# Attention scores from 32 array rows at a time, two heads per 32 value columns, and a block-diagonal state

## The chip, the cores and the metric

The kernel runs on one core of a Trainium2 chip. The metric is the device time of one execution in microseconds (us); the median of three is compared. TensorE, VectorE, ScalarE and GpSimd appear in the profile as PE (its weight loads as PEld), DVE, ACT and POOL; SP issues DMAs.

## What is computed

One decoder block on x of shape (4, 256, 256), all in fp32: linear attention with decay, then a mixture of four experts chosen by token, then a second attention-like layer over the batch index, each followed by a residual and a layer norm. The change is in the first part:

```
q, k = rope(silu(x@Wq)), rope(silu(x@Wk)); v = x@Wv      # 16 heads of 16, chunks of 128
scores  = einsum('bthd,bshd->bhts', qi, ki) * D          # D: causal decay
o_intra = einsum('bhts,bshd->bthd', scores, vi)
o_inter = einsum('bthd,bhde->bthe', qi*decay_q, S)
S_new   = lam_C*S + einsum('bshd,bshe->bhde', ki*decay_k, vi)
x = layernorm(x + (groupnorm(o * sigmoid(gate))*w) @ Wo)
x = layernorm(x + experts(x)); x = layernorm(x + ffn(x))
```

## The kernel before, in words

The 1024 rows of x are 8 tiles of 128, two chunks for each of the four batches. Every engine has its program written out by hand, in rounds, and the engines meet only through counting semaphores: `wait_ge(S_("probs"), n)` holds the engine's queue, with all that stands behind it, until the count is reached. Nothing reorders the work.

Round i of the attention (i from 0 to 10) works at several tiles at once. PE: `transpose_qk(i)`, `attend(i-1)`, in even rounds `make_state`, `proj_qkv(i+1)` (queries and keys together, then values), in round 7 (`MOE_START`) `transpose_h(0)`, the scores of tile i, `transpose_on(i-2)`, `turn_back(i-1)`, `project_o(i-2)`. DVE: `copy_kT(i)`, `gate_o(i-2)` and `norm_o(i-2)` (a chain of some 13 small instructions, of which eleven are the inverse root `newton`/`ors`), in even rounds `decay_state`, a layer norm (`h`), `rope_cos(i+1)` (`rcos`), four `mask_scores` (`probs`) with `rope_add(i+1)` (`qkr`) between the second and the third, `residual1(i-2)` (`x`, `stats`, `agg`). In round 3 and in round 5 DVE also prepares weights of the last part behind its residual (with `f_w`). ACT: `expand_q(i)`, `silu_qk(i+1)`, `copy_v(i+1)`, `copy_oT(i-1)`, `copy_onT(i-2)`.

A score matmul takes all 128 array rows, that is the keys of eight heads, against `qx`, the queries expanded with zeros so that only one head meets its keys; one covers four heads (512 columns). The four of a tile alternate between PSUM banks 3 and 4, so the third needs the first mask, the fourth the second. Values are padded from 16 to 32 columns per head, so outputs and state hold 32 rows or columns per head, half of them zero. `attend` keeps four heads in flight, each in its own 32 array columns, and begins with group g as soon as that group's mask is done. From round 7 on rounds of the experts are mixed in (`expert_up`, `expert_down`; `hTe` and `aTe` are their masked inputs). In round 8 `attend(7)` stands on PE between `expert_up(0)` and `expert_up(1)`.

Of the kernel before, what the change touches and what calls it, by code (L numbers as in the profile page):

```python
# [39 lines left out]
C_CHUNK = C_PARITY + 2  # L40
C_ROPE2 = C_CHUNK + KT
C_TRIL = C_ROPE2 + L * 2 * HK
C_POW = C_TRIL + L * L * H
C_END = C_POW + 1
# [14 lines left out]
def shape_constants():  # L59
# [6 lines left out]
    for f in range(KT):  # L66
        c[:, C_CHUNK + f] = np.exp(-slope * P)[f * (H // KT) + p // HD]

# [19 lines left out]
def decoder_block(nc, x, tokens, ctx, wq, wk, wv, wo, wg1, wg2, norm_w, conv_w, fwq, fwk, fwv, fwg, router, fwout,  # L88
                  consts, out):
    stack = ExitStack()  # L90
    with stack:
# [45 lines left out]
        qx = sb("qx", [P, 2, KT, 8, P])  # L137
        kT = sb("kT", [P, 2, KT, P])
        probs = sb("probs", [P, 2, H, P])
        state = sb("state", [P, KT, D])  # L140
# [24 lines left out]
        after = qx[:, :, :, :, :].rearrange("p b k h n -> p (b k h n)")  # L165
        fq = after[:, 0:1024].rearrange("p (c l n) -> p c l n", c=2, l=L)
        fv = after[:, 2048:4096].rearrange("p (c l n) -> p c l n", c=2, l=L)
# [36 lines left out]
        tril = con[:, C_TRIL:C_TRIL + L * L * H].rearrange("p (l m h) -> p l m h", l=L, m=L)  # L204
        half_neg = con[:, C_POW:C_POW + 1]

# [53 lines left out]
        def _(eng):  # L260
            eng.memset(qx[:, :, :, :, :], 0.0).then_inc(S_("zeros"), 1)
# [206 lines left out]
        def _(eng):  # L468
# [7 lines left out]
            eng.wait_ge(S_("zeros"), 2)  # L476
# [7 lines left out]
            def copy_v(i):  # L484
                eng.wait_ge(S_("v_made"), i + 1)
                if i >= 3:
                    eng.wait_ge(S_("o_made"), i - 2)
                    eng.wait_ge(S_("state_made"), (i - 3) // 2 + 1)
                eng.activation(v_sb[:, i % 3, :, 0:HD], heads(bank[1][:, 0:D]), ACT.Copy).then_inc(S_("v_copied"), 1)

            def expand_q(i):
                eng.wait_ge(S_("qkT_made"), i + 1)
# [3 lines left out]
                for r in range(4):  # L496
                    rr = slice(32 * r, 32 * r + 32)
                    for par in range(2):
                        eng.activation(qx[rr, i % 2, :, 2 * r + par, :], two(bank[2][rr, 0:2 * P]), ACT.Copy,  # L499
                                       scale=con[rr, C_PARITY + par:C_PARITY + par + 1]).then_inc(S_("q_expanded"), 1)  # L500

            def copy_oT(i):
# [3 lines left out]
                eng.activation(oT[:, i % 2, :], bank[5][:, :], ACT.Copy).then_inc(S_("oT_copied"), 1)  # L506
# [125 lines left out]
        def _(eng):  # L632
# [74 lines left out]
            def copy_kT(i):  # L707
                eng.wait_ge(S_("kT_made"), i + 1)
                if i >= 2:
                    eng.wait_ge(S_("scores_made"), 4 * (i - 1))  # L710
                eng.tensor_copy(kT[:, i % 2, :, :], two(bank[7][:, 0:D])).then_inc(S_("kT_copied"), 1)

            def mask_scores(i, g):
                eng.wait_ge(S_("scores_made"), 4 * i + g + 1)
                if i >= 2:
                    eng.wait_ge(S_("o_made"), i - 1)
                eng.tensor_tensor(probs[:, i % 2, 4 * g:4 * g + 4, :],  # L717
                                  bank[3 + g % 2][:, :].rearrange("p (h n) -> p h n", h=4),
                                  causal.unsqueeze(1).to_broadcast([P, 4, P]), ALU.mult).then_inc(S_("probs"), 1)

            def decay_state(b):
# [3 lines left out]
                for f in range(KT):  # L725
# [633 lines left out]
```

## Time and profile before

| | |
|---|---|
| median of three executions | 255.02 us (254.4, 255.02, 258.87) |
| span of the profiled execution, first to last instruction | 256.0 us |
| mean granted TensorE clock, share of full speed | 0.925 |
| busy: PE, DVE, POOL, ACT | 82%, 69%, 45%, 32% of the span |

The profiled execution's own device time is not listed apart; its span lies 1.0 us above the median. "Busy" of PE counts matmuls in flight, so it does not say that PE sets the pace. An fp32 matmul appears as two records, each with a weight load; a transpose is one record. In the timeline, records of one kind are merged, and in brackets stands how long the engine had been idle before and which work ended last ahead of it ("issue" where the profile shows none).

### The profile page before, as it was taken

The page shows a single profiled execution, that of the slowest core. Times are in us where ns is not written, and L with a number is a line of the kernel's source. Part 1 is how long each engine was busy: PE and PEld are TensorE (multiplying, and loading weights), DVE is VectorE, ACT ScalarE, POOL GpSimd, SP SyncE. Part 2 cuts the span into 40 slices and gives each one's busy share as a digit, 9 for nine tenths or more (in the row PEclk, how much of TensorE's full clock was granted, in tenths as well). Part 3 has the DMA queues.
Part 4 walks back from the last instruction along what each step waited for, and adds up shares of the span by engine and source line. Part 5 has one row for each costly group of instructions (what it writes and reads, how often), then busy time and mean ns, then how long its engine had stood idle before and what let it go on. Part 6 is the DMA issues. An engine that isn't in the chain of part 4 may idle for free.

```text
span 256.0 us, 3809 instructions
## 1 busy us (share of the span) xinstructions
PE 209.2 (82%) x1254; PEld 146.0 (57%) x1254; DVE 176.7 (69%) x438; ACT 81.7 (32%) x219; POOL 114.0 (45%) x188
## 2 busy tenths in 40 slices
PE   3788999995987798849799989999999997842461
PEld 1367555562745364515799776686786966411340
DVE  1168848779597979793556863348769788897751
ACT  0075664452432534241100113403223234423021
POOL 9661207335161413140516352346558529656352
PEclk9999999999799999977979999999999999995555
DMA  7990000000000000000000000000000001001011
GB/s 195 339 299 5 3 0 4 0 1 0 3 1 0 3 1 0 3 0 0 3 0 3 1 0 0 3 1 0 0 3 0 0 4 40 3 0 41 0 38 45
DMA packets 7027, 6.65 MB, mean 26 GB/s; under 512 B 1232, under 2 KB 6624, under 8 KB 7008
## 3 DMA queue, kind: packets, MB, share of 16 engines
q1 hardware_dynamic: 5744, 5.33, 6.6%
q10 hardware_dynamic: 1264, 1.08, 1.4%
q8 instruction: 10, 0.16, 0.3%
q14 instruction: 9, 0.07, 0.1%
HBM read 5.36 MB, written 1.05 MB: 25 GB/s over the span
## 4 chain that ended last, share of the span: by engine, by line
PE 52%; DVE 24%; issue 9%; POOL 6%; ACT 4%; DMA 3%; ACTq 1%; DVEq 0%; POOLq 0%
PE bank L1029 19%; PE bank L1230 12%; PE bank L1087 9%; PE bank L1244 4%; PE bank L1024 3%; DMA w_qk<-in_L_attn_Wk 3%; DVE hTe L776 2%; DVE w_qk L937 2%; PE bank L1132 2%; DVE stats L749 1%; POOL rstd L301 1%; DVE newton L685 1%; DVE probs L717 1%; PE bank L1120 1%; DVE newton L684 1%
## 5 line engine op out<-in xcount | busy, mean ns | idle before, releaser
L1087 PE MATMUL bank<-qx,kT 128*128 128x512 f32 x64 | 33.7, 652 | 10.6 <-DVE probs L717 8.9
L1230 PE MATMUL bank<-hTe,ctxT 128*128 128x128 f32 x256 | 31.7, 285 | 2.6 <-issue 2.6
L1230 PEld LDWEIGHTS bank<-hTe,ctxT 128*128 128x128 f32 x256 | 31.0, 201 | 3.2 <-issue 3.1
L499 ACT ACTIVATE qx<-bank,con 32x256 f32<-32x256 f32 x64 | 26.4, 458 | 16.0 <-PE bank L1024 15.4
L1244 PE MATMUL bank<-ctxT,aTe 128*128 128x256 f32 x128 | 29.0, 379 | 0.0
L284 POOL TENSOR_TENSOR rsin<-qk,rope_tab 128x256 f32<-128x256 f32 x16 | 13.2, 845 | 34.9 <-ACT qk L482 34.9
L1029 PE MATMUL bank<-f_w,oT 128*128 128x512 f32 (+4 forms) x80 | 28.0, 496 | 0.8 <-ACT oT L552 0.7
L298 POOL TENSOR_SCALAR rstd<-agg 128x1 f32<-128x1 f32 x24 | 5.3, 222 | 49.3 <-DVE agg L751 48.5
L1087 PEld LDWEIGHTS bank<-qx,kT 128*128 128x128 f32 x64 | 11.7, 197 | 26.8 <-issue 24.5
L717 DVE TENSOR_TENSOR probs<-bank,con 128x512 f32<-128x512 f32 x32 | 21.6, 686 | 5.8 <-PE bank L1087 5.0
L1244 PEld LDWEIGHTS bank<-ctxT,aTe 128*128 128x128 f32 x128 | 23.7, 190 | 2.9
L336 POOL TENSOR_TENSOR aTe<-rcos,mask 128x256 f32<-128x256 f32 x8 | 11.9, 1493 | 25.5 <-DVE rcos L835 25.5
L1029 PEld LDWEIGHTS bank<-f_w,oT 128*128 128x128 f32 x80 | 14.4, 190 | 12.0 <-issue 5.7
L835 DVE TENSOR_TENSOR rcos<-rcos,bank 128x256 f32<-128x256 f32 x8 | 3.4, 420 | 21.7 <-ACT rcos L602 21.7
L1029 PE MATMUL bank<-w_qk,xT 128*128 128x512 f32 x32 | 17.0, 658 | 1.5 <-DMA w_qk<-in_L_attn_Wk 1.5
L301 POOL TENSOR_TENSOR rstd<-rstd,con 128x1 f32<-128x1 f32 x24 | 14.0, 582 | 2.0
L336 POOL TENSOR_TENSOR hTe<-hT,mask 128x512 f32<-128x512 f32 x8 | 13.3, 1656 | 2.6 <-ACT hT L539 2.6
L1024 PE MATMUL bank<-con,fgo 128*128 128x128 f32 x16 | 3.7, 357 | 12.8 <-POOL fgo L414 12.8
L512 ACT ACTIVATE onT<-bank 128x256 f32<-128x256 f32 x8 | 3.1, 384 | 33.8 <-PE bank L1024 33.8
L1029 PE MATMUL bank<-f_out,onT 128*128 128x256 f32 x32 | 11.7, 522 | 1.6 <-ACT onT L592 1.6
L1024 PEld LDWEIGHTS bank<-con,fgo 128*128 128x128 f32 x16 | 2.4, 179 | 15.2 <-POOL fgo L414 14.8
L1111 PE MATMUL bank<-probs,v_sb 128*32 128x128 f32 x256 | 10.8, 274 | 0.0
(128 smaller groups left out, 407.7 us busy)
## 6 DMA issues: line engine op xcount, KB each, us to landing
x_sb<-in_x SPq DMA_DIRECT2D x4, 256.0 KB, 6.8
ctx_sb<-in_ctx SPq DMA_DIRECT2D x1, 1024.0 KB, 12.3
out<-x_sb SPq DMA_DIRECT2D x8, 128.0 KB, 1.7
fgo<-in_itok_BxS ACTq DMA_DIRECT2D x1, 512.0 KB, 9.3
con<-shape_constants SPq DMA_DIRECT2D x1, 338.5 KB, 3.0
w_v<-in_L_attn_Wv SPq DMA_DIRECT2D x1, 256.0 KB, 5.5
w_qk<-in_L_attn_Wq ACTq DMA_DIRECT2D x1, 256.0 KB, 5.7
w_qk<-in_L_attn_Wk ACTq DMA_DIRECT2D x1, 256.0 KB, 7.3
```

The source lines that it names most:

```text
L284: eng.tensor_tensor(dst[:, :, s, :], src[:, :, 1 - s, :], tab[:, :, s, :], ALU.mult)\
L298: eng.tensor_scalar(rstd[:, n, i:i + 1], agg[:, n, i, 1:2], LN_EPS, None, ALU.add)\
L301: eng.tensor_tensor(rstd[:, n, i:i + 1], rstd[:, n, i:i + 1], half_neg, ALU.pow)\
L336: eng.tensor_tensor(dst[:, j % 2, experts[0]:experts[1], :, :], two(src[:, j % 2, :]).unsqueeze(1).to_broadcast([P, n, KT, P]), mask[:, ex ...
L499: eng.activation(qx[rr, i % 2, :, 2 * r + par, :], two(bank[2][rr, 0:2 * P]), ACT.Copy, scale=con[rr, C_PARITY + par:C_PARITY + par + 1]). ...
L717: eng.tensor_tensor(probs[:, i % 2, 4 * g:4 * g + 4, :], bank[3 + g % 2][:, :].rearrange("p (h n) -> p h n", h=4), causal.unsqueeze(1).to_ ...
L1024: last = eng.transpose(dst[:, k * P:(k + 1) * P], src[:, k * P:(k + 1) * P], ident)
L1029: last = eng.matmul(dst, lhsT[:, k, :], w[:, k, :], start=(k == 0), stop=(k == KT - 1))
L1087: eng.matmul(bank[3 + g % 2][:, :], kT[:, i % 2, g // 2, :], qx[:, i % 2, g // 2, 4 * (g % 2):4 * (g % 2) + 4, :].rearrange("p h n -> p (h ...
L1111: last = eng.matmul(bank[5][32 * n:32 * n + 32, g * P:(g + 1) * P], v_sb[:, i % 3, h, :], probs[:, i % 2, h, :], start=(i % 2 == 0), stop= ...
L1230: last = eng.matmul(bank[0][:, f * P:(f + 1) * P], ctxT[:, k, e, f * P:(f + 1) * P], hTe[:, j % 2, e, k, :], start=(e == 0 and k == 0), st ...
L1244: last = eng.matmul(bank[3][:, 0:D], aTe[:, j % 2, e, k, :], ctxT[:, k, e, :], start=(e == 0 and k == 0), stop=(e == E - 1 and k == KT - 1))
```

## The change

- `expand_q` writes two copies of the transposed queries (one for even, one for odd heads of each pair), with 2 instructions on 128 partitions in place of 8 on 32. `qx` shrinks from 8 to 2 planes and needs no clearing; the buffers of the last part that lay over it get a tensor of their own (`after`).
- A score matmul takes the 32 array rows of two heads (strip r, half f) against the two parities (256 columns). There are 8 per tile; strips 0, 1 and 2 write banks 3, 4 and 7 without waiting for a mask of this tile, strip 3 reuses bank 3 behind the first mask.
- Values of two heads share 32 columns (`packed`), so the output and the state are dense: `attend` takes its state part with 4 matmuls of full size in place of 16 of 32 columns, `copy_oT` copies 256 columns, `turn_back` makes two transposes in place of four and puts them in the upper half of bank 5, and `decay_state` is one instruction with a block mask. The table of constants grows by 254 columns.
- Waits: the transposed keys lie in bank 2 beside the queries, so `expand_q` waits for both and `copy_kT` for `expand_q`. The state lies in bank 1 beside the values, so the value projection waits for `decay_state`. `attend` waits for all four masks and for `gate_o` of the tile before, which now stands first in DVE's round.

```diff
             def expand_q(i):
-                eng.wait_ge(S_("qkT_made"), i + 1)
+                eng.wait_ge(S_("kT_made"), i + 1)
...
-                for r in range(4):
-                    rr = slice(32 * r, 32 * r + 32)
-                    for par in range(2):
-                        eng.activation(qx[rr, i % 2, :, 2 * r + par, :], two(bank[2][rr, 0:2 * P]), ACT.Copy,
-                                       scale=con[rr, C_PARITY + par:C_PARITY + par + 1]).then_inc(S_("q_expanded"), 1)
+                for par in range(2):
+                    eng.activation(qx[:, i % 2, :, par, :], two(bank[2][:, 0:D]), ACT.Copy,
+                                   scale=con[:, C_PARITY + par:C_PARITY + par + 1]).then_inc(S_("q_expanded"), 1)
...
             def copy_kT(i):
                 eng.wait_ge(S_("kT_made"), i + 1)
+                eng.wait_ge(S_("q_expanded"), 2 * i + 2)
...
             def decay_state(b):
...
-                for f in range(KT):
-                    eng.tensor_scalar(state[:, f, :], bank[7][:, f * D:(f + 1) * D], con[:, C_CHUNK + f:C_CHUNK + f + 1],
-                                      None, ALU.mult).then_inc(S_("state"), 1)
+                eng.tensor_tensor(state[:, :], bank[1][:, D:2 * D], chunk_decay, ALU.mult).then_inc(S_("state"), 1)
...
             def attention_round(i):
+                if 0 <= i - 2 < TILES:
+                    gate_o(i - 2)
                 if i < TILES:
                     copy_kT(i)
...
-                if i >= 3:
-                    eng.wait_ge(S_("gated"), i - 2)
+                if i:
+                    eng.wait_ge(S_("state"), (i + 1) // 2)
                 project(bank[1][:, 0:D], xt, w_v[:, :, :]).then_inc(S_("v_made"), 1)
...
+            def score_rows(i, r, f):
+
+                rr = slice(32 * r, 32 * r + 32)
+                return eng.matmul(score_bank(r)[:, f * D:(f + 1) * D], kT[rr, i % 2, f, :],
+                                  qx[rr, i % 2, f, :, :].rearrange("p h n -> p (h n)"), start=True, stop=True)
...
+                for f in range(KT):
+                    for r in range(3):
+                        last = score_rows(i, r, f)
+                        if f == KT - 1:
+                            last.then_inc(S_("scores_made"), 1)
+                eng.wait_ge(S_("probs"), 4 * i + 1)
+                for f in range(KT):
+                    last = score_rows(i, 3, f)
+                last.then_inc(S_("scores_made"), 1)
...
             def attend(i):
...
-                    eng.wait_ge(S_("oT_copied"), i)
+                    eng.wait_ge(S_("gated"), i)
```

On PE, from the state matmuls of tile 4 to the scores of tile 6, which is round 6 up to its scores. Before:

```order
L1120 MATMUL bank<-v_sb,qkr 128x256 [waits v_copied,kT_copied]
L1120 MATMUL bank<-v_sb,qkr 128x256
L1029 MATMUL bank<-w_qk,xT 128x512 [waits qk_silu]
L1029 MATMUL bank<-w_qk,xT 128x512
L1029 MATMUL bank<-w_v,xT 128x256 [waits gated,v_copied]
L1029 MATMUL bank<-w_v,xT 128x256
L1087 MATMUL bank<-qx,kT 128x512 [waits probs,kT_copied,q_expanded] x4
```

And in the changed kernel:

```order
L1142 MATMUL bank<-v_sb,qkr 128x128 [waits v_copied]
L1142 MATMUL bank<-v_sb,qkr 128x128
L1040 MATMUL bank<-w_qk,xT 128x512 [waits qk_silu]
L1040 MATMUL bank<-w_qk,xT 128x512
L1040 MATMUL bank<-w_v,xT 128x256 [waits state,v_copied]
L1040 MATMUL bank<-w_v,xT 128x256
L1091 MATMUL bank<-qx,kT 128x256 [waits probs,kT_copied,q_expanded]
L1091 MATMUL bank<-qx,kT 128x256 x5
L1091 MATMUL bank<-qx,kT 128x256 [waits probs]
L1091 MATMUL bank<-qx,kT 128x256
```

The value projection (`w_v`) now waits for DVE's `state` of the same round, and the last two score matmuls for the first mask.

On PE in round 8, `attend(7)` between the experts' first up-projection and their second. Before, its last two groups of heads and what follows:

```order
L1106 MATMUL bank<-qx,state 32x128 [waits probs]
L1106 MATMUL bank<-qx,state 32x128 x3
L1111 MATMUL bank<-probs,v_sb 32x128 x4
L1106 MATMUL bank<-qx,state 32x128 [waits probs]
L1106 MATMUL bank<-qx,state 32x128 x3
L1111 MATMUL bank<-probs,v_sb 32x128 x4
L1024 MATMUL bank<-con,h 128x128 [waits hT_copied,h1_done]
L1024 MATMUL bank<-con,h 128x128
L1230 MATMUL bank<-hTe,ctxT 128x128 [waits activated,hTe_pool,hTe_vector]
```

And in the changed kernel, from `expert_up(0)` (the first two rows) to `expert_up(1)` (the last):

```order
L1246 MATMUL bank<-hTe,ctxT 128x128 [waits qk_silu,hTe_pool,hTe_vector]
L1246 MATMUL bank<-hTe,ctxT 128x128 x15
L1129 MATMUL bank<-qx,state 128x128 [waits state,probs,v_copied,gated]
L1129 MATMUL bank<-qx,state 128x128
L1133 MATMUL bank<-probs,v_sb 32x128 x8
L1129 MATMUL bank<-qx,state 128x128 x2
L1133 MATMUL bank<-probs,v_sb 32x128 x8
L1035 MATMUL bank<-con,h 128x128 [waits probs,hT_copied,h1_done]
L1035 MATMUL bank<-con,h 128x128
L1246 MATMUL bank<-hTe,ctxT 128x128 [waits activated,hTe_pool,hTe_vector]
```

`attend` (L1129, L1133; its first state matmul waited for `state,probs,v_copied,oT_copied` before) has changed the wait on ACT's copy for `gated`; everything below it on PE's queue waits with it. What it waits for stands on DVE, in the changed kernel, at the change from round 7 to round 8:

```order
L846 TENSOR_TENSOR rcos<-rcos,bank 128x256 [waits z_silu]
L786 TENSOR_TENSOR aTe<-rcos,mask 128x768 [waits activated]
L786 TENSOR_TENSOR hTe<-hT,mask 128x512 [waits hT_copied]
L744 TENSOR_TENSOR og<-bank,gate 128x256 [waits o_normed,o_back]
L765 TENSOR_SCALAR h<-x,agg,rstd 128x256 [waits ln0_rstd]
L748 TENSOR_TENSOR osq<-og 128x256 [waits gated]
```

`og` (`gate_o`) stands one instruction earlier than before, ahead of `h`, but still behind the three expert instructions.

## Rows read from the trace of the kernel before

**Rows 1.** The page: granted clock (tenths) and DMA rate in 40 slices; the constants' DMA.
```profile
PEclk9999999999799999977979999999999999995555
GB/s 195 339 299 5 3 0 4 0 1 0 3 1 0 3 1 0 3 0 0 3 0 3 1 0 0 3 1 0 0 3 0 0 4 40 3 0 41 0 38 45
...
con<-shape_constants SPq DMA_DIRECT2D x1, 338.5 KB, 3.0
```

**Rows 2.** Timeline, DVE in round 5: start us, us, engine, line, operation.
```profile
81.99 0.42 DVE L762 TENSOR_TENSOR x<-bank,x_sb 128x256 f32<-128x256 f32 x1 [1.13 <-PE bank L1029]
...
83.33 0.41 DVE L733 TENSOR_TENSOR og<-bank,gate 128x256 f32<-128x256 f32 x1
...
89.12 1.27 DVE L717 TENSOR_TENSOR probs<-bank,con 128x512 f32<-128x512 f32 x2
...
93.75 0.42 DVE L762 TENSOR_TENSOR x<-bank,x_sb 128x256 f32<-128x256 f32 x1 [1.13 <-PE bank L1029]
```

**Rows 3.** Timeline, PE and ACT in round 5.
```profile
82.21 3.37 ACT L499 ACTIVATE qx<-bank,con 32x256 f32<-32x256 f32 x8 [1.44 <-PE bank L1024]
...
86.02 1.88 PE L1087 MATMUL bank<-qx,kT 128*128 128x512 f32 x4
...
89.94 1.96 PE L1087 MATMUL bank<-qx,kT 128*128 128x512 f32 x4 [2.04 <-DVE probs L717]
...
92.58 1.13 PE L1029 MATMUL bank<-w_o,onT 128*128 128x256 f32 x4
```

**Rows 4.** Timeline, round 6 up to its first mask, PE and DVE.
```profile
94.08 0.43 PE L1106 MATMUL bank<-qx,state 128*32 128x128 f32 x8
...
96.66 0.41 DVE L733 TENSOR_TENSOR og<-bank,gate 128x256 f32<-128x256 f32 x1
96.79 1.13 PE L1120 MATMUL bank<-v_sb,qkr 128*128 128x256 f32 x4 [0.76 <-DVE kT L711]
...
97.76 1.88 PE L1029 MATMUL bank<-w_qk,xT 128*128 128x512 f32 x4
...
100.19 0.87 DVE L726 TENSOR_SCALAR state<-bank,con 128x256 f32<-128x256 f32 x2
100.34 1.88 PE L1087 MATMUL bank<-qx,kT 128*128 128x512 f32 x4
...
102.43 1.27 DVE L717 TENSOR_TENSOR probs<-bank,con 128x512 f32<-128x512 f32 x2
```

**Rows 5.** Timeline, rounds 3 and 4: late scores, residual, gate, first mask.
```profile
61.84 1.27 DVE L717 TENSOR_TENSOR probs<-bank,con 128x512 f32<-128x512 f32 x2
62.66 2.38 PE L1087 MATMUL bank<-qx,kT 128*128 128x512 f32 x4 [2.83 <-DVE probs L717]
...
67.85 0.42 DVE L762 TENSOR_TENSOR x<-bank,x_sb 128x256 f32<-128x256 f32 x1 [2.09 <-PE bank L1029]
...
71.22 0.41 DVE L733 TENSOR_TENSOR og<-bank,gate 128x256 f32<-128x256 f32 x1
...
77.35 1.27 DVE L717 TENSOR_TENSOR probs<-bank,con 128x512 f32<-128x512 f32 x2
```

**Rows 6.** Half-microsecond windows: busy of PE, PEld, DVE, ACT, POOL, granted clock, DMA.
```profile
64.50:65.00 0.50, 0.50 (x2) 0.16 (x1) 0.00 (x0) 0.00 (x0) 0.00 (x0) 0.50 0.00 0
```

**Rows 7.** Timeline, DVE and PE at the change from round 0 to round 1.
```profile
33.28 1.46 DVE L717 TENSOR_TENSOR probs<-bank,con 128x512 f32<-128x512 f32 x2
...
34.37 1.08 PE L1111 MATMUL bank<-probs,v_sb 128*32 128x128 f32 x32
```

**Rows 8.** Timeline, rounds 7 and 8.
```profile
120.64 3.74 PE L1230 MATMUL bank<-hTe,ctxT 128*128 128x128 f32 x32
...
124.31 0.43 PE L1106 MATMUL bank<-qx,state 128*32 128x128 f32 x8
...
126.16 1.22 DVE L776 TENSOR_TENSOR hTe<-hT,mask 128x512 f32<-128x512 f32 x1
...
128.60 5.44 PE L1230 MATMUL bank<-hTe,ctxT 128*128 128x128 f32 x32 [1.97 <-issue]
```

More of the change, by code:

```diff
@@ L136, in decoder_block @@
         v_sb = sb("v_sb", [P, 3, H, 32])
-        qx = sb("qx", [P, 2, KT, 8, P])
+        qx = sb("qx", [P, 2, KT, 2, P])
+        after = sb("after", [P, 3 * L * D])
         kT = sb("kT", [P, 2, KT, P])
         probs = sb("probs", [P, 2, H, P])
-        state = sb("state", [P, KT, D])
+        state = sb("state", [P, D])
         oT = sb("oT", [P, 2, 512])
@@ L1099, in attend @@
                 if i % 2:
-                    eng.wait_ge(S_("state"), 2 * (i // 2) + 2)
-                for g in range(4):
-                    eng.wait_ge(S_("probs"), 4 * i + g + 1)
+                    eng.wait_ge(S_("state"), i // 2 + 1)
+                eng.wait_ge(S_("probs"), 4 * i + 4)
+                for f in range(KT):
+                    out = bank[5][:, f * P:(f + 1) * P]
                     if i % 2:
-                        for n in range(4):
-                            h = 4 * g + n
-                            eng.matmul(bank[5][32 * n:32 * n + 32, g * P:(g + 1) * P],
-                                       state[:, h // 8, 32 * (h % 8):32 * (h % 8) + 32],
-                                       qx[:, i % 2, h // 8, h % 8, :], start=True, stop=False)
-                    for n in range(4):
-                        h = 4 * g + n
-                        last = eng.matmul(bank[5][32 * n:32 * n + 32, g * P:(g + 1) * P], v_sb[:, i % 3, h, :],
-                                          probs[:, i % 2, h, :], start=(i % 2 == 0), stop=True)
+                        for par in range(2):
+                            eng.matmul(out, state[:, f * P:(f + 1) * P], qx[:, i % 2, f, par, :],
+                                       start=(par == 0), stop=False, skip_group_check=True)
+                    for par in range(2):
+                        for r in range(4):
+                            last = eng.matmul(out[32 * r:32 * r + 32, :], v_sb[:, i % 3, 8 * f + 2 * r + par, :],
+                                              probs[:, i % 2, 4 * r + 2 * f + par, :],
+                                              start=(i % 2 == 0 and par == 0), stop=(par == 1), skip_group_check=True)
                 last.then_inc(S_("o_made"), 1)
@@ L1116, in make_state @@
                 i = 2 * b
-                eng.wait_ge(S_("kT_copied"), i + 1)
                 eng.wait_ge(S_("v_copied"), i + 1)
                 for f in range(KT):
-                    last = eng.matmul(bank[7][:, f * D:(f + 1) * D], qkr[:, i % 2, D + f * P:D + (f + 1) * P],
-                                      v_sb[:, i % 3, 8 * f:8 * f + 8, :].rearrange("p h e -> p (h e)"),
-                                      start=True, stop=True)
+                    last = eng.matmul(bank[1][:, D + f * P:D + (f + 1) * P], qkr[:, i % 2, D + f * P:D + (f + 1) * P],
+                                      packed(v_sb[:, i % 3, 8 * f:8 * f + 8, :]), start=True, stop=True)
                 last.then_inc(S_("state_made"), 1)
@@ L1127, in turn_back @@
                 eng.wait_ge(S_("oT_copied"), i + 1)
-                eng.wait_ge(S_("v_copied"), min(i + 3, TILES))
-                if i:
-                    eng.wait_ge(S_("gated"), i)
-                for g in range(4):
-                    last = eng.transpose(bank[1][:, g * P:(g + 1) * P], oT[:, i % 2, g * P:(g + 1) * P], ident)
-                last.then_inc(S_("o_back"), 1)
+                transpose2(bank[5][:, D:2 * D], oT[:, i % 2, 0:D]).then_inc(S_("o_back"), 1)
             proj_qkv(0)
@@ L1170, in attention_round @@
                 if i < TILES:
-                    for g in range(4):
-                        scores(i, g)
+                    scores(i)
                 if 0 <= i - 2 < TILES:
```

69 lines of the change are left out of this document (37 added, 32 removed).

## The prediction

> **What bounds the kernel now.** I read the page first: PE is busy 82% of the span, DVE 69%, and PE's clock is full except in a few slices [rows 1]. The shares don't say what the change is worth, so I read the timeline of the attention, round by round, for what each engine waits for. From round 3 on it is one loop between DVE and PE. X is where the residual `x` starts, M where the first mask starts. In round 5 [rows 2]: X at 81.99, M at 89.12, the next X at 93.75. From X to M (7.13) DVE works almost without a gap: statistics, gate, inverse root, layer norm, `rcos`. From M to X (4.63) PE sets the time: it has been idle 2.04 us for the first mask [rows 3], then come two scores of 512 columns, a transpose and its copy, and the output projection from 92.58, and DVE waits 1.13 us for it. So the scores made ahead of M cost nothing there, those behind M all of their time, and every instruction on DVE ahead of M costs its own.
>
> **Late scores: a gain in each round.** Behind M stand 2 matmuls of 512 columns, 0.86 us each (four records from 89.94 to 91.65, [rows 3]). In their place come 2 of 256 columns in the same array strip, which can't run together: half, 0.86 in all. Nothing else of the path from M to X changes: the two transposes saved in `turn_back` (0.22) lie beside ACT's copy of `onT`. So M to X shrinks by 0.86, and DVE still waits 0.3 at X, since its four masks and `qkr` are done some 3.5 us after M.
>
> **Early scores.** Six matmuls of 256 columns in three strips. If the strips run together they take 0.86, one after another 2.57. Column strips do run together here: 16 matmuls of 32 columns by 128 take 1.08 us [rows 7], where one after another, at 0.86 x 128/512 = 0.21 each, they would take 3.4. Row strips appear nowhere in this trace. Their weights are 128 columns wide and each fp32 matmul loads twice; the nearest row is `expert_up`, 32 pairs of a 128-column load and a 128-column pass in 3.67 us (120.64 to 124.31, [rows 8]), 0.115 a pair. I can't tell load from pass in it, so a load is at most 0.115. Twelve loads in sequence bound the six at 1.4. I take 1.3 (the first mask can start 1.1 after the first of them, plus 0.2 for the hand-over) and keep both ends.
>
> The Trainium skill (TensorEngine Tiling (Array Packing), Key Properties) says that different tiles can load and multiply in parallel; by that rule it is 0.86, a rival below. TensorE: Matmul & The Clock Gate, LDWEIGHTS, says that a load costs its columns whatever its rows, a 32x128 load as much as a 128x128 one. That speaks for 1.3. No row here shows either alone.
>
> **The query copies and the order on DVE.** ACT's eight `qx` instructions take 3.37 us [rows 3], two of them 0.84. They start 0.22 later, behind the transposes of k, so are done 1.3 us after X; the gate stands first and fills DVE until about then. `copy_kT` behind it costs no more than ahead of it. Zero in odd rounds. The 3.37 us are hidden today, since scores wait for M, so their saving is worth nothing in itself.
>
> **Even rounds 4 and 6: two new waits on PE.** `attend` now waits for the gate, and the value projection for the state. Round 6, counted from X at 93.75 ([rows 4]). The gate now starts where `kT` did, 0.34 ahead of 96.66, so at X+2.6, and ends at X+3.0 (the extra weights of the last part stand before it). Attend takes 1.9 (94.08 to 96.79 less 0.76 idle), to X+4.95; its state part is 4 full matmuls of 0.21 for 4 groups of 0.22, no difference. `make_state` halves, 0.97 to 0.48, X+5.4. Queries and keys 1.72, X+7.15. On DVE the inverse root ends and `state` starts at X+6.45 (3.53 behind the gate, plus 0.34 for `kT`), ends X+6.9, 0.45 sooner for being one instruction; so the value wait is just covered. Values 0.86, X+8.0. Scores 1.1 + 0.1, hand-over 0.2: M at X+9.5, against 8.68 today (102.43). So +0.8, less 0.86 behind M. In round 4 the same sum with the gate at X+3.0 (71.22 - 67.85 less 0.34) gives M at X+9.95 against 9.5 [rows 5]: +0.45, less 0.86. Together -0.5. If the six scores took 2.57, the first mask would wait for four of them, 1.71, +0.6 in each round.
>
> **Odd rounds.** Rounds 5 and 7: -0.86 each, -1.7. Round 3: -0.86, and the clock. Today PE idles 2.83 us before the late scores, and then works at 0.50 of the clock, the 1.2 GHz level [rows 6], so that M to X is 6.01 in place of 4.63 [rows 5]. With the gate wait, the idle time is split into 1.2 and 2.4, and I take that the fall stays out there: -1.4. Round 3: -2.3.
>
> **Rounds 0 to 2,** where PE is the busier one: in round 0 `copy_kT` waits for ACT (1.1 us where the transposes alone took 0.2), the four `ctxT` copies behind it slide by 0.9, and behind them state, values (they wait for it), scores and masks. Then `attend(0)`, which starts at 34.37 while two masks run [rows 7], waits for all of them, until 34.75. Packed scores give back 1.71 - 1.2 in each. I reckon M of round 2 at 1.2 late, and 0.86 back behind it: +0.3.
>
> **Round 8: the dearest new wait.** Today `attend(7)` runs from 124.31, in the shadow of DVE's and POOL's masked inputs, and `expert_up(1)` starts at 128.60. Now it waits for `gate_o(6)`, which stands on DVE behind `hTe` (126.16 + 1.22) and ends at 127.85. Attend 1.9, two transposes 0.2: `expert_up(1)` at 130.0, +1.4 [rows 8]. It is on the path, and behind it so is everything.
>
> **Constants.** 254 more columns, 130 KB, at the 339 GB/s of the start [rows 1] 0.4 us, ahead of the weights that PE waits for: +0.3. GpSimd loses the clearing of `qx`, which nothing waits for, 0.
>
> **Clock lost elsewhere.** The new idle stretches are about 3.1 and 2.7 us before attend in rounds 4 and 6 and 3.5 in round 8, against the 2.83 that cost 1.4. In round 8 `expert_up(1)` ran slow already (5.44 against 3.67), so there the fall only changes its victim. For rounds 4 and 6 I charge one fall, +1.3.
>
> **The sum:** +0.3 - 2.3 - 0.5 - 1.7 + 1.4 + 0.3 + 1.3 = -1.2. Against the profiled span, 256.0 - 1.2 = 254.8; it lies 1.0 above the median, so **253.8**.
>
> **Rivals.**
> - Strips load and multiply at once, and the clock holds. Early scores 0.86 in place of 1.3, in the five rounds 0, 1, 2, 4 and 6: -2.0; no charge for the clock, -1.3; and round 8 keeps the full clock, so the 1.8 of the slow `expert_up(1)` comes back in part, -0.9. 249.6. For it: the column strips. Against it: longer idle stretches than today.
> - The strips don't run together (the change doesn't do what it says): +0.6 to +0.7 in those five rounds, +3.2: 257.0. For it: no row shows row strips. Against: column strips do.
> - The other side: the gate wait cools PE. What counts is not the wait but the work behind it: attend, `make_state`, `qk` and values (5 us at full speed) stand right behind the idle stretch and ahead of M. Let the clock fall at each of the waits of rounds 4, 6 and 8 and in round 3 again, each for the 1.4 that round 3 shows today: rounds 4 and 6 2.8 in place of the 1.3 charged, +1.5; round 3 +1.4; round 8 +1.4 if `expert_up(1)` stays slow as well. +4.3: 258.1. It decides at the length of the stretch: behind 2.83 us the fall came [rows 5, 6], behind the 2.04 of round 5 [rows 3] it didn't, and the new ones are 2.7 to 3.5.
>
> **How the numbers follow.** Forecast 253.8 at 0.5, its own range 251.5 to 256 (0.1 a round either way in the hand-overs, one fall of the clock more or less). Fast rival 0.2, no overlap 0.13, cold PE 0.17. The range 249.3 to 258.6 leaves out the tails beyond the outer rivals. A measurement of this kernel tells about 2%, 5.1 us, from no change (its three runs span 4.5): faster by that is below 249.9, most of the fast rival and no more, 0.15; slower is above 260.1, half of the cold rival and a little of the others, 0.1; within 0.75.
>
> **What the profile after would show.** Late scores 0.86 behind M and X 3.8 behind M; six early scores in 1.3 (0.86 and 2.57 are the rivals); PE idle 3 us before attend in rounds 4 and 6, put down to `og`; M 9.5 and 9.95 behind X there; `attend(7)` at 127.8 less what was gained, released by `og`; ACT 2.5 us less per tile with no change of time from it. It would be wrong if the experts' part moved by more than the shift at its start, or if the masks became the bound behind M.

## The result and the profile after

The changed kernel took **269.42 us** (median; 267.03 to 270.87) against 254.82 (254.4 to 258.87) of the kernel before on the same chip, a ratio of **1.054** [1.045, 1.062]: slower, outside the range of 249.3 to 258.6. The profiled execution took 268.65 with a span of 266.8, against 256.0 before. Executions of one kernel differ by up to 3%, and a ratio counts only those within 1.5% of the kernel's fastest, so medians over all executions stand beside the ratios. The span of 256.0 belongs to the longest of the first three executions of the kernel before (258.87; the other two, 254.4 and 255.02, are shorter than that span, while in all other runs here the device time is 1.7 to 3.0 longer than the span). So "before" in a trace stands for a long execution, at a mean clock of 0.925, where later executions of this kernel have 0.921 to 0.945, most of them above 0.93.

The page of the changed kernel: PE's busy share and clock in 40 slices, and three groups of instructions (busy us, mean ns | idle before them and its releaser):

```profile
PE   2798887987668886874949999899999998761552
...
PEclk9999979779779777978688999999999999995657
...
L1091 PE MATMUL bank<-qx,kT 32*128 32x256 f32 x128 | 19.1, 408 | 11.1 <-DVE probs L730 10.6
...
L1129 PE MATMUL bank<-qx,state 128*128 128x128 f32 x32 | 8.5, 411 | 9.3 <-DVE og L744 9.3
...
L1133 PE MATMUL bank<-probs,v_sb 128*32 128x128 f32 x256 | 13.0, 350 | 2.8 <-DVE og L744 2.2
```

Two things are new against [rows 1]. The clock has dips in every round, from slice 6 on; in the first three of these slices PE is busy for 80% or more. And `attend` (L1129, L1133) waits 11.5 us for `og`.

The whole attention in windows (busy of PE, PEld, DVE, ACT, POOL, then the granted clock), after:

```profile
22.00:142.00 120.00, 93.92 (x634) 63.09 (x633) 80.01 (x202) 21.45 (x51) 35.70 (x60) 0.83 0.00 1
```

and before:

```profile
22.00:128.00 106.00, 90.92 (x677) 55.55 (x675) 80.50 (x191) 43.10 (x100) 34.78 (x59) 0.95 0.00 1
```

DVE's busy time is the same and ACT's is halved, as meant; PE's busy time grew although it has less to do, since it works at 0.83 of its clock in place of 0.95. In half-microsecond windows from 22 us to the end of the experts' second up-projection (145.85, before 134.04) I count those that read below 0.75: 11 stretches (36 to 39, 46 to 49.5, 56.5 to 59.5, 70 to 73.5, 77 to 80 and so on), 40.0 us in all; before it was 3, from 64.0, 112.0 and 129.0, 13.5 us in all. The 26.5 us more cost at most half their length, 13.3.

The first of them is in round 0. Timeline, PE and DVE:

```profile
31.95 1.14 PE L1091 MATMUL bank<-qx,kT 32*128 32x256 f32 x12
33.12 1.29 DVE L730 TENSOR_TENSOR probs<-bank,con 128x512 f32<-128x512 f32 x2 [1.01 <-PE bank L1091]
33.86 1.13 PE L1091 MATMUL bank<-qx,kT 32*128 32x256 f32 x4 [0.77 <-DVE probs L730]
...
36.35 1.93 PE L1133 MATMUL bank<-probs,v_sb 128*32 128x128 f32 x32 [0.64 <-DVE probs L730]
```

and windows of the scores and of what follows:

```profile
31.50:35.00 3.50, 2.72 (x19) 1.48 (x17) 2.49 (x5) 0.38 (x1) 1.84 (x2) 1.00 0.00 0
...
36.00:39.00 3.00, 2.65 (x33) 2.01 (x34) 0.63 (x2) 0.59 (x2) 0.00 (x0) 0.50 0.00 0
```

The scores ran at full clock, six matmuls in the same 1.14 us as the late two (1.13): the strips run together, and the first mask started 1.17 after the first of them. Then the clock fell, and `attend(0)` took 1.93 for what took 1.08 before [rows 7]. The idle stretches around it are new but short: 1.18 us at 27.3 (0.35 before), 0.77 and 0.64, where the kernel before idled for 2.04 us in round 5 and kept its clock [rows 1], [rows 3].

Rounds 3 and 4:

```profile
68.19 1.13 PE L1091 MATMUL bank<-qx,kT 32*128 32x256 f32 x4 [2.31 <-DVE probs L730]
...
70.16 2.08 PE L1040 MATMUL bank<-w_o,onT 128*128 128x256 f32 x4 [0.25 <-ACT onT L524]
...
72.28 0.42 DVE L772 TENSOR_TENSOR x<-bank,x_sb 128x256 f32<-128x256 f32 x1 [1.74 <-PE bank L1040]
...
75.30 0.41 DVE L744 TENSOR_TENSOR og<-bank,gate 128x256 f32<-128x256 f32 x1
...
75.77 0.71 PE L1129 MATMUL bank<-qx,state 128*128 128x128 f32 x4 [2.68 <-DVE og L744]
```

The late scores shrank as forecast, but the output projection behind them took 2.08 in place of 1.13 [rows 3], so M to X is 4.82 in round 3 and 5.02 in round 5, where 3.8 was forecast. Round 8:

```profile
130.20 4.32 PE L1246 MATMUL bank<-hTe,ctxT 128*128 128x128 f32 x32
...
137.44 0.41 DVE L744 TENSOR_TENSOR og<-bank,gate 128x256 f32<-128x256 f32 x1
...
137.91 0.94 PE L1129 MATMUL bank<-qx,state 128*128 128x128 f32 x4 [3.39 <-DVE og L744]
...
142.11 3.74 PE L1246 MATMUL bank<-hTe,ctxT 128*128 128x128 f32 x32
```

`attend(7)` stands behind `og`, and with two transposes it takes 4.2 us, most of it at 0.50 of the clock. The second up-projection starts 13.5 later than before (142.11 against 128.60 [rows 8]); 2.7 of it come back from there on: 1.7 in the up-projection itself, which took 3.74 in place of 5.44, since the third stretch of before lay on it, and the rest behind it, where the clock stood higher in two of the last four slices (5657 against 5555).

### The profile page after: what moved, and what is told of

Its sections match the earlier page's. It is cut to its first block, busy times and chain, and to the rows that moved or that the text cites. A ratio compares the mean times of both kernels' runs of the same rounds, so it can differ in the third digit from the quotient of the medians.

```text
span 266.8 us, 3622 instructions
## 1 busy us (share of the span) xinstructions
PE 210.1 (79%) x1206; PEld 151.5 (57%) x1206; DVE 171.9 (64%) x434; ACT 60.4 (23%) x171; POOL 111.0 (42%) x187
## 3 DMA queue, kind: packets, MB, share of 16 engines
q10 hardware_dynamic: 1264, 1.08, 1.3%
## 4 chain that ended last, share of the span: by engine, by line
PE 53%; DVE 24%; POOL 7%; issue 7%; ACT 4%; DMA 3%; ACTq 1%; DVEq 0%; POOLq 0%
PE bank L1040 21%; PE bank L1246 11%; PE bank L1091 5%; PE bank L1035 4%; PE bank L1260 4%; PE bank L1133 3%; PE bank L1129 3%; DMA w_qk<-in_L_attn_Wk 3%; DVE probs L730 3%; DVE w_qk L948 2%; DVE hTe L786 2%; POOL rstd L313 2%; DVE stats L759 1%; ACT onT L524 1%; DVE rcos L707 1%
## 5 line engine op out<-in xcount | busy, mean ns | idle before, releaser
L296 POOL TENSOR_TENSOR rsin<-qk,rope_tab 128x256 f32<-128x256 f32 x16 | 14.3, 913 | 48.6 <-ACT qk L494 48.6
L1246 PE MATMUL bank<-hTe,ctxT 128*128 128x128 f32 x256 | 30.5, 278 | 0.2 <-issue 0.2
L1091 PE MATMUL bank<-qx,kT 32*128 32x256 f32 x128 | 19.1, 408 | 11.1 <-DVE probs L730 10.6
L348 POOL TENSOR_TENSOR aTe<-rcos,mask 128x256 f32<-128x256 f32 x8 | 11.9, 1493 | 27.9 <-DVE rcos L846 27.9
L730 DVE TENSOR_TENSOR probs<-bank,con 128x512 f32<-128x512 f32 x32 | 20.5, 682 | 4.4 <-PE bank L1091 4.4
L1091 PEld LDWEIGHTS bank<-qx,kT 32*128 32x128 f32 x128 | 11.5, 188 | 17.7 <-DVE probs L730 13.8
L1129 PE MATMUL bank<-qx,state 128*128 128x128 f32 x32 | 8.5, 411 | 9.3 <-DVE og L744 9.3
L1040 PE MATMUL bank<-w_o,onT 128*128 128x256 f32 x32 | 14.4, 597 | 1.5 <-ACT onT L524 1.2
L1133 PE MATMUL bank<-probs,v_sb 128*32 128x128 f32 x256 | 13.0, 350 | 2.8 <-DVE og L744 2.2
L348 POOL TENSOR_TENSOR hTe<-hT,mask 128x512 f32<-128x512 f32 x8 | 13.3, 1658 | 1.4 <-ACT hT L551 1.4
L1129 PEld LDWEIGHTS bank<-qx,state 128*128 128x128 f32 x32 | 6.3, 278 | 11.8 <-DVE og L744 10.4
L707 DVE TENSOR_TENSOR rcos<-qk,rope_tab 128x512 f32<-128x512 f32 x8 | 6.5, 808 | 10.0 <-ACT qk L494 10.0
## 6 DMA issues: line engine op xcount, KB each, us to landing
x_sb<-in_x SPq DMA_DIRECT2D x4, 256.0 KB, 7.7
w_v<-in_L_attn_Wv SPq DMA_DIRECT2D x1, 256.0 KB, 6.4
w_qk<-in_L_attn_Wq ACTq DMA_DIRECT2D x1, 256.0 KB, 6.4
w_qk<-in_L_attn_Wk ACTq DMA_DIRECT2D x1, 256.0 KB, 8.0
```

Source lines behind the costliest of these rows:

```text
L296: eng.tensor_tensor(dst[:, :, s, :], src[:, :, 1 - s, :], tab[:, :, s, :], ALU.mult)\
L348: eng.tensor_tensor(dst[:, j % 2, experts[0]:experts[1], :, :], two(src[:, j % 2, :]).unsqueeze(1).to_broadcast([P, n, KT, P]), mask[:, ex ...
L707: eng.tensor_tensor(rcos[:, i % 2, :], qk[:, i % 2, :], rope_tab[:, i % 2, 0, :], ALU.mult)\
L730: eng.tensor_tensor(probs[:, i % 2, 4 * g:4 * g + 4, :], score_bank(g)[:, :].rearrange("p (h n) -> p h n", h=4), causal.unsqueeze(1).to_br ...
L1040: last = eng.matmul(dst, lhsT[:, k, :], w[:, k, :], start=(k == 0), stop=(k == KT - 1))
L1091: return eng.matmul(score_bank(r)[:, f * D:(f + 1) * D], kT[rr, i % 2, f, :], qx[rr, i % 2, f, :, :].rearrange("p h n -> p (h n)"), start= ...
```

## Experiments

Two theories stood before the first of these runs: **rows**, that matmuls over few array rows let the clock fall; **wait**, that the new wait of `attend` for `og` does, as the cold-PE rival had it.

### Both kernels with the other's score matmuls

The changed kernel, with matmuls over all 128 rows in place of strips:

```diff
-                return eng.matmul(score_bank(r)[:, f * D:(f + 1) * D], kT[rr, i % 2, f, :],
-                                  qx[rr, i % 2, f, :, :].rearrange("p h n -> p (h n)"), start=True, stop=True)
+                return eng.matmul(score_bank(r)[:, f * D:(f + 1) * D], kT[:, i % 2, f, :],
+                                  qx[:, i % 2, f, :, :].rearrange("p h n -> p (h n)"), start=True, stop=True)
```

> The changed kernel with each group of 32-row score matmuls replaced by one matmul of all 128 rows and the same 256 columns: two early (four in round 0), two late. It leaves out part of the scores (banks 4 and 7 keep old values, heads are mixed), with all masks, waits and later work in place, so its time stands for the same schedule with full array rows. Theory A (32-row matmuls count too little as work, and the clock falls behind them): the clock stays near 1.0 in rounds 0 to 2, falls at most in rounds 3, 4, 6, 7 and 8 behind the long waits, mean clock at or above 0.92, time 256 to 261. Theory B (the falls come from the new idle stretches): the same falls as the changed kernel, mean clock 0.86 to 0.89, time 267 to 270.

The kernel before, with its score matmuls over 32 rows:

```diff
-                eng.matmul(bank[3 + g % 2][:, :], kT[:, i % 2, g // 2, :],
-                           qx[:, i % 2, g // 2, 4 * (g % 2):4 * (g % 2) + 4, :].rearrange("p h n -> p (h n)"),
+                eng.matmul(bank[3 + g % 2][:, :], kT[0:32, i % 2, g // 2, :],
+                           qx[0:32, i % 2, g // 2, 4 * (g % 2):4 * (g % 2) + 4, :].rearrange("p h n -> p (h n)"),
```

> The kernel before, with its four score matmuls per tile over array rows 0 to 31 in place of all 128 (it leaves out three quarters of each sum); columns, order and waits as before. Theory A: the clock falls in most rounds of the attention, mean clock below 0.90, time 262 or more against 255. Theory B: nothing changes, 255 and clock 0.925.

And the same over 64 rows (`kT[0:64]`, `qx[0:64]`), run later:

> The kernel before with its four score matmuls per tile over array rows 0 to 63 (half of each sum left out). Rows in flight: between, 259 to 264, clock 0.89 to 0.91. Only the lone strip: 255, clock 0.925.

Measured: full rows in the changed kernel 259.81 (254.54 to 262.2), ratio to the kernel before 1.001 [0.993, 1.009]. That ratio rests on three executions of ten; the medians over all, 259.81 and 256.93, give 1.011. So four fifths of the loss or more are gone. 32 rows in the kernel before 269.25 (267.65 to 270.0), 1.049 [1.040, 1.057]; 64 rows 262.86, 1.027 [1.019, 1.034]. Nothing else was touched there: instructions, columns, waits and order are those of the kernel before. Round 1 of the 32-row version, windows of its eight score records and of what follows:

```profile
38.50:42.40 3.90, 3.88 (x10) 1.27 (x9) 3.27 (x5) 0.96 (x3) 3.56 (x6) 1.00 0.00 0
...
43.00:46.00 3.00, 3.00 (x45) 2.53 (x47) 1.90 (x6) 2.21 (x6) 0.86 (x3) 0.50 0.03 8
```

PE was busy for 3.88 of the 3.90 us and without a gap in the second, and the clock stood at 0.50 there, where the kernel before has 1.00. That shows **rows**: fewer rows in the scores, and nothing else, give the kernel before a loss of the size of the change, and with 64 rows a good half of it stays (0.027 of 0.049).

The full-row version settles round 0 as well. It has nearly the same idle stretches there as the changed kernel, and `attend(0)` behind them took 1.08:

```profile
33.95 1.13 PE L1090 MATMUL bank<-qx,kT 128*128 128x256 f32 x4 [0.79 <-DVE probs L730]
...
36.44 1.08 PE L1132 MATMUL bank<-probs,v_sb 128*32 128x128 f32 x32 [0.63 <-DVE probs L730]
```

Rounds 0 to 2 in one window, the changed kernel and then the one with full rows:

```profile
22.00:62.00 40.00, 33.44 (x238) 22.03 (x236) 24.78 (x53) 9.66 (x21) 10.55 (x18) 0.87 0.00 1
...
22.00:62.00 40.00, 32.36 (x226) 21.84 (x224) 28.41 (x64) 10.89 (x24) 14.46 (x28) 1.00 0.00 1
```

The full-row trace is of one of its longest executions (262.07), and still shows no dip there; its dips come from 64 us on.

### The gate moved ahead of the next residual

`gate_o` of a tile goes behind the four masks of the round before, so that `attend` finds it done:

```diff
             def attention_round(i):
-                if 0 <= i - 2 < TILES:
+                if i == TILES + 1:
                     gate_o(i - 2)
...
+                if 1 <= i < TILES:
+                    gate_o(i - 1)
                 if 0 <= i - 2 < TILES and i < TILES:
                     residual1(i - 2)
```

> The changed kernel with gate_o of tile i-1 moved into round i, between the masks and the residual, where DVE waits for PE, so that attend does not wait for it. Theory A: the waits for og (11.5 us in all) go, 4 to 7 us come back, and the falls of the clock behind the scores stay: 262 to 265, clock below 0.91. Theory B (idle stretches and these waits are the whole of it): the long idle stretches before attend are gone and with them most falls, 253 to 257.

And with the full-row matmuls as well:

> The early gate with every score matmul over all 128 rows, 256 columns, two early (four in round 0) and two late; it leaves out part of the scores, as the run with full rows did. It bounds what a full array and the early gate are worth together: 247 to 251 if the clock is what is left of the loss after the early gate; 259 to 262 if it is not.

Measured: 260.85 (259.34 to 264.57), 1.015 [1.002, 1.028]; with full rows 255.24 (252.12 to 258.73), 0.994 [0.989, 0.998]. So the wait costs time too, some 10 us by the ratios (1.054 to 1.015), but the two don't add: full rows alone give 12 to 13.5 back, the gate alone some 10, both some 15. Most of the dips stay in the version with the gate alone (34.5 us in place of 40.0, by the same windows), without any wait for `og`. What became late next is the wait that the prediction had found just covered: the value projection for `state`:

```profile
78.63 2.04 PE L1042 MATMUL bank<-w_v,xT 128*128 128x256 f32 x4 [2.70 <-DVE state L738]
```

### TensorE alone

A kernel with no other work: PE multiplies without a pause, 28 steps of 256 columns with all rows, then 28 steps of each kind (one strip of 32 rows; three; four; one of 64; two of 64; four column strips), with 28 full steps between them.

> TensorE alone: phases of 28 fp32 matmuls of 128 rows by 256 columns (12 us), and between them phases of as many steps of 1, 3, 4 strips of 32 rows, 1 and 2 strips of 64 rows, and 4 strips of 32 columns. It computes nothing of the block. Theory A: the granted clock falls to 0.5 in the phase of one 32-row strip although PE is never idle, and stays 1.0 with 4 strips and with 2 of 64 rows; 3 strips and 1 of 64 rows show where between. Theory B: 1.0 throughout. Strips in flight together: 28 steps of 3 or 4 take about the 12 us of the full phases; if loads come one after another, 28 x 6 x 0.107 = 18 us for three and 24 us for four.

Windows inside the phases, in that order (busy of PE, PEld, POOL, then the clock):

```profile
26.00:46.00 20.00, 20.00 (x48) 15.04 (x47) 0.00 (x0) 0.51 0.00 1
57.00:69.00 12.00, 12.00 (x166) 10.73 (x161) 0.00 (x0) 1.00 0.01 3
81.00:93.00 12.00, 12.00 (x225) 11.34 (x224) 0.00 (x0) 1.00 0.01 3
106.00:118.00 12.00, 12.00 (x57) 10.14 (x56) 0.00 (x0) 1.00 0.01 1
130.00:142.00 12.00, 12.00 (x111) 10.69 (x112) 0.00 (x0) 1.00 0.00 1
155.00:166.00 11.00, 11.00 (x212) 6.62 (x208) 0.00 (x0) 1.00 0.01 3
```

One strip alone took the clock to 0.51 although PE is never idle. Three and four strips make 166 and 225 records in the time of 57, so they run fully side by side, weight loads too, and keep the clock. The Trainium skill (TensorEngine Tiling (Array Packing), Key Properties) says that different tiles load and multiply in parallel; this trace agrees. The Trainium skill (TensorE: Matmul & The Clock Gate, What's actually happening) has the gate follow how busy PE is; the first window differs from that, PE busy all the time at 0.51, and the measurement decides.

Mixtures, also without a pause: two strips and two in turn; one and three; one and two; three times one strip and then a full matmul; two and two.

> TensorE never idle, computing nothing of the block: phases of 32 steps of 256 columns between full phases of 28, with 2 strips of 32 rows in each step (mean 64 rows), 1 and 3 in turn (64), 1 and 2 in turn (48), three steps of 1 to one full (56), two of 1 to two full (80). By rows in flight the clock falls first in the phase of 48 and stays in that of 80; if only a lone strip counts too little, the first phase stays at 1.0 and those with many lone strips fall (the fourth before the third).

```profile
22.00:34.00 12.00, 12.00 (x114) 10.65 (x114) 0.00 (x0) 1.00 0.01 1
48.00:60.00 12.00, 12.00 (x116) 10.71 (x115) 0.00 (x0) 1.00 0.01 1
80.00:96.00 16.00, 16.00 (x57) 12.92 (x55) 0.00 (x0) 0.50 0.00 0
120.00:136.00 16.00, 16.00 (x34) 10.16 (x35) 0.00 (x0) 0.50 0.00 0
147.00:161.00 14.00, 14.00 (x54) 8.91 (x54) 0.00 (x0) 1.00 0.01 1
```

The clock follows the mixture, not its emptiest part: one strip and three hold it as two and two do, one and two don't. The last window shows one cost more, which the forecast left out: 54 records in 14.00 us at full clock, where full rows alone would make some 66 (57 in 12.00), so a step from a strip to full rows or back costs some 0.2 us (an estimate, 27 steps of 0.52 for 0.43 with a passage at every second). In the changed kernel the first score starts 0.96 behind the value projection (40.53 to 41.49), with full rows 0.86 (39.27 to 40.13): small beside the clock.

A third kernel of this kind, bursts of two steps and a wait for DVE between them, was to show the same with idle time:

> TensorE in bursts of two steps of 256 columns (0.86 us), each followed by a wait for one small VectorE instruction (some 0.6 us), 16 bursts to a phase; it computes nothing of the block. Phases of full rows stand between phases of 4, 3 and 2 strips of 32 rows in flight, one of 64 rows, one of 32 rows. If the monitor counts rows in flight: full rows and 4 strips keep 1.0, one strip falls to 0.5, 2 strips and 64 rows behave alike (fall), 3 strips in between. If it counts instructions or time in flight: all phases alike.

It tells nothing on rows. Already its full-row bursts took 2.07 us. In the blocks above four such records take 1.13 behind a wait at full clock (`w_o` [rows 3]) and 2.08 at 0.50 (70.16):

```profile
9.27 2.07 PE L132 MATMUL bank<-x_sb 128*128 128x256 f32 x4 [0.59 <-DVE junk L118]
```

so by its durations it ran at the low level from its start, and there was nothing to fall from.

### Which of the scores

Strips 0 and 1 ahead of the first mask and 2 and 3 together behind it, in place of three and one:

```diff
-                    for r in range(3):
+                    for r in range(2):
                         last = score_rows(i, r, f)
...
-                    last = score_rows(i, 3, f)
-                last.then_inc(S_("scores_made"), 1)
+                    for r in range(2, 4):
+                        last = score_rows(i, r, f)
+                        if f == KT - 1:
+                            last.then_inc(S_("scores_made"), 1)
```

> The changed kernel with the strips of 32 rows issued in two pairs: strips 0 and 1 early (banks 3 and 4), strips 2 and 3 together behind the first mask (banks 7 and 3), so that no strip is ever alone in the array. Late time unchanged (two steps of 256 columns). If the lone strip is what lets the clock fall: most of the 12 to 14 us come back, 257 to 262. If strips count by rows, as the fewer rows early take back what the late ones give (0.43 us x 3 + 0.86 x 1 against 0.86 x 2 + 0.86 x 2 of row time): 266 to 270, as the changed kernel. If only idle stretches count: 269.

and with the early gate:

> Both edits: strips in pairs and gate_o(i-1) ahead of the residual of round i. If each repairs a cause of its own: 250 to 256, faster than either alone (260.9 for the early gate). If the pairs repair nothing: 259 to 262.

Only the late two over all rows:

```diff
                 for f in range(KT):
-                    last = score_rows(i, 3, f)
+                    last = full_rows(i, 3, f)
```

> The changed kernel with only the two late matmuls over all 128 rows (their scores mix heads), the six early strips as they are: the six leave 96 of 128 rows busy. If the lone late strip is the cause: 255 to 261, as with full rows everywhere (fast runs 255). If the early strips count too little as well: 263 to 268.

Measured: pairs 269.11 (267.9 to 271.32), 1.052 [1.043, 1.060], no change from three and one; with the early gate 262.56 (258.08 to 263.32), no interval, against 260.85 with three and one. Late full rows 258.58 (257.69 to 259.91), 1.011 [1.006, 1.016]. So two matmuls in a tile make some 11 us of the loss (0.043 of 0.054), but sharing the same strips out more evenly gives nothing, as one and three held the clock as two and two did on TensorE alone.

Can the late pair be filled up with zeros? The queries of strip 3 are copied once more with the other rows set to zero, and the late matmuls take all rows, with the early gate. First with the keys' copy held behind two more ACT instructions, then with that off the path (the second copy made from `qx`):

```diff
+                for par in range(2):
+                    eng.activation(qz[:, i % 2, :, par, :], two(bank[2][:, 0:D]), ACT.Copy,
+                                   scale=con[:, C_LAST + par:C_LAST + par + 1]).then_inc(S_("q_last"), 1)
...
-                    last = score_rows(i, 3, f)
+                    last = eng.matmul(score_bank(3)[:, f * D:(f + 1) * D], kT[:, i % 2, f, :],
+                                      qz[:, i % 2, f, :, :].rearrange("p h n -> p (h n)"), start=True, stop=True)
```

> The changed kernel with the early gate, and strip 3 computed over all 128 rows against queries that are zero outside rows 96 to 127 (two more ACT instructions per tile); the six early strips as they are. If the lone strip is the main cause and the early gate the other: 250 to 255. If zeros count as no activity, or the early strips count too little: 257 to 261.

> The changed kernel with the early gate and strip 3 over all 128 rows against zero-padded queries, which ACT now makes from qx in SBUF, so that the keys' copy does not wait for them. If padded rows count as full and the first try lost its time on the keys' copy: 253 to 257. If zeros do not count: 260 to 262, the clock below 0.91.

259.92 (259.49 to 262.68), 1.014 [1.009, 1.019], no better than 1.015 of the early gate alone; the second 258.35 (253.54 to 258.93), unclear. The clock did gain. Rounds 0 to 2 of the early gate alone, then of the first padded version:

```profile
22.00:62.00 40.00, 34.32 (x246) 22.19 (x244) 25.97 (x58) 10.26 (x22) 12.26 (x24) 0.91 0.00 1
...
22.00:62.00 40.00, 32.21 (x254) 20.69 (x252) 27.05 (x61) 13.71 (x32) 14.22 (x27) 1.00 0.01 1
```

The second padded version has 1.00 there too, as has the one with late full rows. The windows below 0.75, counted as above, fall from 34.5 us to 20.0 and 24.5. That the time hardly followed goes with longer waits in the first padded version: 15.2 us for the masks ahead of the late scores in place of 11.9, and 5.5 for `state` in place of 3.4; no run separates them. So rows that meet zeros seem to count for the clock. The kernel before speaks for it as well: seven eighths of its `qx` are zeros, and it holds the clock where 32 rows don't.

### The early gate in the kernel before

The same move of `gate_o` in the kernel before; then also the packed values, the dense state and output and the two transposes of the change, but scores over all rows, the dense state left in bank 7 and a plain copy of the queries for it in odd tiles:

> The kernel before with nothing changed but gate_o(i-1) ahead of the residual of round i, where DVE waits 1.1 us for PE. 0.33 to 0.42 us less of DVE ahead of the first mask in rounds 3 to 7: 252.5 to 254 against 255. If DVE is not what sets X to M: no change.

> The early gate in the kernel before, plus the packed values and the dense state of the change, laid out so that no wait is added: state in the upper half of bank 7, turned outputs in the upper half of bank 1, scores over 128 rows as before. decay_state is one instruction (0.45 less in four rounds on DVE), make_state halves, turn_back makes two transposes. If the useful half of the change is there: 1 to 2 us below the kernel with only the early gate, 251 to 253. If the shorter PE work opens the way for the clock to fall: 254 to 258.

253.51 (250.33 to 254.74), 0.981 [0.975, 0.988], and 251.41 (249.91 to 252.63), 0.980 [0.975, 0.985]. Both lie about 2% below the kernel before, whose median there was 256.89, with intervals clear of 1. Whether the packing adds to the gate is unclear: the ratios are the same, but they leave out three of the gate's six executions and none of the packed ones; the medians over all lie 2.1 us apart (its expectation was 1 to 2). The clock's line of the first:

```profile
PEclk9999999999999999999999999999999999985757
```

No dip is left in the attention of this execution, but it is the fastest of the six (250.33, mean clock 0.961; the others have 0.931 to 0.946), and it stands against a long one of the kernel before, so it shows the best case and not the typical one. Apart from the clock, X comes earlier: X to X is 10.94 in round 5 (80.06 to 91.00) where it was 11.76. The gate's 0.41 now stands where DVE waits for the output projection anyway (that wait went from 1.13 to 0.74), and the other 0.4 is what is left of longer and shorter small instructions (two of the inverse root took 0.59 and 0.65 before and 0.17 each now, `h` 0.40 before and 0.82 now).

### The sum over the runs

For each version: how much later (or earlier) than 134.04 the second up-projection ends, and half of what it has more (or less) than the 13.5 us of windows below 0.75 up to there, both from its profiled execution:

| version | later, us | half of the low time |
|---|---|---|
| changed kernel | 11.8 | 13.3 |
| changed, pairs | 12.3 | 13.0 |
| before, 32 rows | 9.6 | 12.0 |
| before, 64 rows | 4.9 | 5.3 |
| changed, full rows | 5.0 | 6.8 |
| changed, late full rows | 2.9 | 3.8 |
| changed, early gate | 3.6 | 10.5 |
| changed, pairs, early gate | 1.0 | 5.3 |
| changed, padded, early gate | 3.0 | 3.3 |
| changed, padded off the path, early gate | 1.9 | 5.5 |
| changed, full rows, early gate | -5.0 | -3.5 |
| before, early gate | -6.9 | -6.8 |
| before, packed, early gate | -7.9 | -5.0 |

The two agree within 3 us in ten of thirteen. The three others all have the early gate in the changed kernel: part of their low time lies under waits (2.7 us of one for `state`, above), and the saved wait for `og` goes against it. The changed kernel is 11.8 later at the end of the up-projection and not 13.5, since the third stretch of the kernel before lay on it. The table is an account, not a proof: half is exact only where PE sets the pace, and each row is one execution.

## Why the prediction was wrong

**The step that failed** is "Clock lost elsewhere", with its "For rounds 4 and 6 I charge one fall, +1.3", and the "I take that the fall stays out there" of round 3. It looked for the clock's falls in idle stretches alone. The runs showed that the matmuls' rows count: 8 more falls, some 13 us, the first three of them in rounds 0 to 2, which hold no idle stretch above 1.2 us and no dip with full rows (1.00 in place of 0.87). No row of the kernel before could give the size, since all its score matmuls have 128 rows; but none excluded it either, and the prediction held the clock to be safe wherever PE was busy.

Its other terms, as later or earlier at X or at the end of the part:

| term | forecast | measured |
|---|---|---|
| constants and start (`rcos(0)`) | +0.3 | +0.9 (22.28 to 23.15) |
| rounds 0 to 2, X of round 2 | +0.3 | +4.7 |
| round 3 | -2.3 | -1.1 |
| rounds 4 and 6 | -0.5 +1.3 | +2.3 +2.9 |
| rounds 5 and 7 | -1.7 | -0.1 -0.1 |
| round 8 | +1.4 | +4.1 |
| sum at the second up-projection | -1.2 | +13.5 |

- **Late scores:** the 0.86 was there (1.13 for four records against 1.96 [rows 3]), and was taken back right behind by the output projection at half pace. In round 7 they gained nothing themselves: behind 3.51 us of waiting they took 2.07. In rounds 5 and 7 that leaves 0.1 of 0.86.
- **Early scores:** the first mask came 1.17 behind the first score, for 1.3; the fast rival was right that loads and passes run together, and wrong that the clock would hold.
- **Query copies:** ACT's `qx` now take 0.84, and the saving was worth nothing, as forecast.
- **The wait for `state`:** just covered, as forecast (0.2 us), and no longer so once the gate was early (2.70).
- **The wait for `og`:** named, at its place, but its idle stretches of 2.4 to 3.4 us were priced with an attend at full clock behind, and one fall for both rounds. M came 11.8 and 11.35 behind X in rounds 4 and 6, for 9.95 and 9.5.
- **Round 8** had the right mechanism and the wrong size: `attend(7)` with its two transposes took 4.2 for the 2.1 reckoned, and `og` ended 7.8 behind X for 7.2.
- **The cold-PE rival** had the direction, with 0.17, and little more than a quarter of the size (4.3 above the forecast, where 15.6 were measured), since it cooled PE by the wait. That wait is the second cause (some 10 us by its removal), not the first.
- **The chance of a time above 260.1** was 0.1 because its only mechanism was bounded by rows in which all matmuls were full. A new shape of instruction on the engine whose clock varies was a case of its own.

## What to carry to other kernels

A matmul over few array rows cost the same time here and counted for less of the work that holds TensorE's clock (1.00 with 128 rows, 0.51 with one strip of 32): before splitting rows, look whether enough strips run at once over the whole stretch, remainders behind a wait above all, and judge the change by the clock of what comes next, not by its own duration. Where a consumer waits for a small instruction at the head of another engine's round, see whether that instruction fits behind the last work of the round before: here this one move was worth about 2% of the kernel before, and what packing adds to it is unclear (0 to 2 us).

## What the runs showed of the hardware

- One 32-row strip after another holds TensorE at 0.51 of its clock, the 1.2 GHz level, with the engine never idle; three or four at once, or one of 64 rows after another, run at 1.00.
- In the kernel before, 128, 64 and 32 rows in the same four matmuls a tile gave ratios of 1, 1.027 and 1.049.
- Rows that meet zeros seem to count: with the lone strip padded to 128 rows the clock was 1.00 from 22 to 62 us in both versions, 0.91 without.
- Passing between a 32-row strip and full rows costs some 0.2 us (an estimate from 54 records in 14.00 us against 57 in 12.00, full clock in both).
- Row strips overlap in full, weight loads included: 225 records of four strips in the 12.00 us that hold 57 of one.
- The clock shown as 1.00 isn't a record of full pace in every trace: in the pulsed kernel it reads 1.00 from start to end, while four records of 256 columns take 2.07 us throughout. TensorE alone shows it too: full rows make 11 records from 8 to 12 us and 21 from 14 to 18, both at a shown 1.00. Durations decide.
